# Six of eight setup stages moved into the attention loop of a one-core transformer block, and the softmax shift split into two factors

## The reference, cut to what matters

```python
def attention(x, Wqkv_w, Wqkv_b, U, Wo_w):        # x: (1, 4096, 256), 16 heads of 16
    proj = quant4(x) @ ternary_weight(Wqkv_w).T + Wqkv_b
    q = proj.reshape(B, N, h, dk).transpose(0, 2, 1, 3)
    k = proj.reshape(B, h, N, dk)
    v = proj.reshape(B, h, N, dk)
    q, k = rotary(q, N), rotary(k, N)
    att = einsum('bhnr,bhmr->bhnm', q @ U, k @ U) / sqrt(dk)
    y = (softmax(att) @ v).transpose(0, 2, 1, 3).reshape(B, N, d)
    return quant4(y) @ ternary_weight(Wo_w).T
x = layernorm(x + attention(x))
x = layernorm(x + ffn(x))                         # silu gate, two gelu layers of 1024, back to 256
```

## Time and profile before

| | |
|---|---|
| median of 3 runs | 2857.3 us (2856.99 to 2858.01) |
| the profiled execution, its own time | 2857.96 us |
| its span (first to last instruction) | 2856.3 us |
| granted TensorE clock, mean | 0.966 of full speed |
| busy: PE / DVE / ACT / POOL | 88% / 21% / 74% / 11% of the span |
| setup, up to the first score matmul | 0 to 262.4 us |
| attention, up to the last sum | 262.4 to 2144.8 us |
| check of the sums and feed-forward part | 2144.8 to 2856.3 us |

### The profile page before, as it was taken

One profiled execution on the slowest core, in us unless ns is written; L12 is line 12 of the kernel. 1 busy time (PEld: TensorE's weight loads), 2 busy tenths in 40 slices (PEclk: granted clock), 3 DMA queues, 4 the chain that ended last, 5 costly groups with the idle time before them and its releaser, 6 DMA issues.

```text
span 2856.3 us, 40002 instructions
## 1 busy us (share of the span) xinstructions
PE 2508.4 (88%) x15895; PEld 1048.4 (37%) x15895; DVE 610.1 (21%) x1164; ACT 2124.8 (74%) x2360; POOL 311.4 (11%) x277
## 2 busy tenths in 40 slices
PE   2432999999999999999999999999995999999998
PEld 2220222222222222222222222222224888888887
DVE  7870000000000000000000000000005555655653
ACT  1222999999999999999999999999992223222232
POOL 2442888500000000000000000000000000000000
PEclk9765999999999999999999999999997999999999
DMA  1438444433333233323323333332222011001100
GB/s 60 130 119 228 103 99 104 93 64 63 64 63 67 58 63 63 71 64 63 62 58 67 64 64 63 69 66 60 59 45 48 1 23 22 22 0 22 22 8 16
DMA packets 94888, 178.42 MB, mean 62 GB/s; under 512 B 30432, under 2 KB 56064, under 8 KB 94208
## 3 DMA queue, kind: packets, MB, share of 16 engines
q1 hardware_dynamic: 90624, 153.05, 24.8%
q0 software_dynamic: 4096, 23.07, 3.0%
HBM read 150.63 MB, written 25.43 MB: 62 GB/s over the span
## 4 chain that ended last, share of the span: by engine, by line
ACT 34%; issue 32%; PE 25%; DVE 6%; DMA 2%; SPq 1%; ACTq 1%; DVEq 0%
ACT PB L270 34%; PE PS L517 16%; PE PS L502 4%; PE PS L529 2%; DVE TD L1060 1%; DMA KSL<-KSD 1%; ACTq L268 1%; PE PS L909 1%; DVE xq L1045 0%; DVE rq L1065 0%; DVE rq L1064 0%; DVE V L1048 0%; DVE khl L1068 0%; SPq L763 0%; DMA QSD<-shr 0%
## 5 line engine op out<-in xcount | busy, mean ns | idle before, releaser
L270 ACT ACTIVATE PB<-PS 128x1024 f32<-128x1024 f32 x2048 | 1877.7, 1237 | 1.4 <-PE PS L236 1.4
L245 PE MATMUL PS<-PB,V 128*17 128x512 f32 x8192 | 1079.3, 599 | 0.3 <-ACT PB L270 0.3
L236 PE MATMUL PS<-QSL,KSL 49*128 49x512 f32 x4096 | 753.6, 446 | 171.1 <-DMA KSL<-KSD 52.3
L236 PEld LDWEIGHTS PS<-QSL,KSL 49*128 49x128 f32 x4096 | 306.0, 185 | 1113.3 <-ACT PB L270 1060.9
L280 DVE STREAM_TRANSPOSE accS<-PS 128x512 f32<-128x512 f32 x32 | 22.9, 717 | 1874.5 <-PE PS L245 1874.5
L592 ACT ACTIVATE hfr<-PS,s 128x512 f32<-128x512 f32 x128 | 86.8, 689 | 300.5 <-PE PS L517 300.4
L245 PEld LDWEIGHTS PS<-PB,V 128*17 128x17 f32 x8192 | 136.0, 95 | 378.6 <-issue 364.1
L517 PE MATMUL PS<-hidden_ar,wh1r 128*128 128x512 f32 x1024 | 237.5, 391 | 0.0
L517 PE MATMUL PS<-hidden_br,wh2r 128*128 128x512 f32 x1024 | 235.3, 390 | 0.0
L517 PEld LDWEIGHTS PS<-hidden_br,wh2r 128*128 128x128 f32 x1024 | 191.7, 188 | 39.4
L517 PEld LDWEIGHTS PS<-hidden_ar,wh1r 128*128 128x128 f32 x1024 | 190.7, 188 | 40.1 <-DVE hfr L681 0.5
(11 more groups left out here) (135 smaller groups left out, 954.2 us busy)
## 6 DMA issues: line engine op xcount, KB each, us to landing
KSL<-KSD SPq DMA_DIRECT2D x256, 256.0 KB, 4.3
KSL<-KSD SPq DMA_DIRECT2D x256, 128.0 KB, 5.0
yq<-in_mlp POOLq DMA_DIRECT2D x44, 256.0 KB, 3.1
QSL<-QSD SPq DMA_DIRECT2D x64, 132.0 KB
QSD<-qhl SPq DMA_DIRECT2D x32, 256.0 KB
KSD<-khl SPq DMA_DIRECT2D x64, 128.0 KB
xg<-in_x SPq DMA_DIRECT2D x8, 512.0 KB, 5.7
QSL<-QSD SPq DMA_DIRECT2D x64, 64.0 KB
```

The costliest lines, as they stand in the source:

```text
L236: ins = pe.matmul(PS[:, 2 * (pair % SLOTS) + e, :], KSL[r, q % 2, s, k * P:(k + 1) * P], QSL[r, b % 2, s, :], start=True, stop=True, tile_ ...
L245: ins = pe.matmul(ACC[i * VW:i * VW + DK + 1, :], V17[:, HT * h + u, c, :], PB[:, (2 * unit + i // 2) % RING, (i % 2) * QW:(i % 2 + 1) * Q ...
L270: act.activation(PB[:, pair % RING, :], PS[:, slot:slot + 2, :].rearrange("p a b -> p (a b)"), ACT.Exp).then_inc(at["probs_ready"], 1)
```

## The change

Groups 0 and 1 are set up as before the attention, and of group 2 the projection, of group 3 the transposed x. The rest is cut into 65 visits and put into the units 6 to 94 of the attention's first query chunk, at most one visit in a unit: on PE between the scores and the sums of the unit. A visit fills one PSUM bank; DVE reads it. Before the attention seven banks are used in turn, in it only bank 7, so that PE waits in each visit until DVE has read the one before.

DVE takes over the copies `qTb`, `rkT` and the higher parts of `qhl` and `khl` from ACT. Squares and root go; ACT takes |.| of the higher parts instead (128x1024, twice a group), which PE sums. The shift becomes this sum for the query row (stored at once) times a constant of the head, -0.04 times the largest such sum of its keys, which goes to a new row of `KSD` and from there by DMAs of its own (`load_consts`) to row 48 of each half of `KSL`. The memsets of `KSL` go. Queries are rotated after the keys' visit KN or KM, no longer right after the projection. Blocks of heads 1, 2, 3 load their first keys late (`KEYS_AT`). The weights come in 44 pieces between the checks, after the last visit.

```diff
+BEFORE = [(XT, 0, 0)]
+for _g in range(2):
+    BEFORE += [(PR, 0, _g), (PR, 1, _g), (XT, 0, _g + 1), (KT_, 0, _g), (KT_, 1, _g), (KG, 0, _g), (KG, 1, _g),
+               (KN, 0, _g)] + [(KM, 0, _g)] * (_g % 2) + [(QT_, 0, _g), (QT_, 1, _g), (QN, 0, _g)]
+BEFORE += [(PR, 0, 2), (PR, 1, 2), (XT, 0, 3)]
+for _g, _u in zip(range(2, NQ), range(-2, 100, 15)):
+    _at = [(_u, PR, 0, _g), (_u + 1, PR, 1, _g), (_u + 4, XT, 0, _g + 1), (_u + 8, KT_, 0, _g), (_u + 9, KT_, 1, _g),
+           (_u + 10, KG, 0, _g), (_u + 11, KG, 1, _g), (_u + 13, KN, 0, _g), (_u + 14, KM, 0, _g), (_u + 17, QT_, 0, _g),
+           (_u + 18, QT_, 1, _g), (_u + 21, QN, 0, _g)]
...
+KEYS_AT, CONSTS_AT = {1: 26, 2: 57, 3: 86}, {1: 29, 2: 60, 3: 89}
...
+        BANKS = (7, 0, 1, 2, 3, 4, 5)
+        bank_number = {use: BANKS[use % len(BANKS)] if use < len(BEFORE) else 7 for use in USE.values()}
...
+        def setup_pe(pe, what, i, g):
+            use = USE[what, i, g]
+            bank = PS[:, bank_number[use], :]
+            if bank_before[use] >= 0:
+                pe.wait_ge(setup_read, bank_before[use] + 1)
...
+        def setup_act(act, what, i, g):
+            if what == KG and i == 1:
+                act.wait_ge(k_high, 2 * g + 2)
...
+                act.activation(sqk[:, :, :], khl[:, 0, :, :].bitcast(F32), ACT.Abs).then_inc(k_abs, 1)
...
+        def setup_dve(v, s, what, i, g):
...
+            v.wait_ge(setup_full, use + 1)
...
+            elif what == PR:
...
+                if i == 1:
...
+                                    ALU.add).then_inc(proj_saved, 1)
+                    v.wait_ge(proj_saved, g + 1)
+                    if g + 1 < NQ:
+                        quantise(v, s, g + 1)
+            elif what == KT_:
+                v.tensor_copy(rkT[:, i, :], bank).then_inc(setup_read, 1)
+            elif what in (KG, QT_):
...
+                v.tensor_copy(hl[:, 0, i, :], bank).then_inc(high, 1)
+                v.wait_ge(high, 2 * g + i + 1)
+                v.tensor_tensor(hl[:, 1, i, :], bank, hl[:, 0, i, :].bitcast(F32), ALU.subtract).then_inc(setup_read, 1)
...
+                if g % 2 == 0:
+                    rotate_queries(v, s, g)
+            elif what == KM:
...
+                v.tensor_scalar(kcr[:, :], ones[0:H, :], kmp[:, H:H + 1], -SHIFT, ALU.mult, ALU.mult).then_inc(consts_ready, 1)
+                rotate_queries(v, s, g)
...
+        def first_pe(pe, at):
+            units = NB_ALL * KT
+            pe.wait_ge(setup_read, len(BEFORE))
...
+            for unit in range(units):
+                pe.wait_ge(at["probs_ready"], 2 * unit + 2)
+                for pair in (2 * unit + 3, 2 * unit + 4):
+                    if pair < 2 * units:
+                        scores_pe(pe, at, 0, pair)
+                if unit in SETUP_AT:
+                    setup_pe(pe, *SETUP_AT[unit])
+                if unit % KT == 0:
+                    pe.wait_ge(at["acc_saved"], unit // KT + 1)
+                sums_pe(pe, at, unit, unit // KT % NBLK)
+        def first_act(act, at):
...
+                if pair % 2 and (pair - 5) // 2 in SETUP_AT:
+                    setup_act(act, *SETUP_AT[(pair - 5) // 2])
...
-            for e in range(2):
-                v.memset(KSL[64 * e + 32:64 * e + 64, :, :, :].bitcast(F32), 1.0).then_inc(slots_set, 1)
...
-            load_weights(pool, True)
...
+            for n in range(WCHUNKS):
+                piece, ready = weight_piece(True, n)
+                pool.dma_start(piece, a["mlp"][:, n * QW:(n + 1) * QW]).then_inc(ready, 16)
```

More of the change, by code:

```diff
@@ L222, in postln_block, with keys_in @@
         K_DVE_F = {True: 50, False: 25}
+        def keys_in(at, n0, q):
+            b, k = divmod(q, QPB)
+            if at is first:
+                return b * 160 + (96 if k < 2 else 160)
+            return n0 * (QPB * 32) + (q // 2 + 1) * 64
         def scores_pe(pe, at, n0, pair):
@@ new lines, in quantise @@
+        def quantise(v, s, g):
+            m = mx[:, g % 2, :, :]
+            src = xg[:, g % 2, :, :]
+            v.wait_ge(x_in[g % 2], 16 * (g // 2) + 16)
+            s.did(v.tensor_reduce(m[:, 0, :], src, AX.X, ALU.max, apply_absolute_value=True))
+            s.settle()
+            maxima(v, s, m)
+            for i in range(TQ):
+                ins = v.tensor_scalar(xq[:, i, :], src[:, i, :], m[:, 1, i:i + 1], 7.0, ALU.mult, ALU.mult)
+            ins.then_inc(x_used, 1)
+            v.wait_ge(x_used, g + 1)
+            if g:
+                v.wait_ge(setup_full, USE[XT, 0, g - 1] + 1)
+            v.tensor_scalar(qb[:, :, :], xq[:, :, :], ROUND, -ROUND, ALU.add, ALU.add).then_inc(q_ready, 1)
+            v.wait_ge(q_ready, g + 1)
@@ new lines, in first_act @@
+        def first_act(act, at):
+            for pair in range(2 * NB_ALL * KT):
+                act.wait_ge(at["scores_ready"], pair + 1)
+                if pair >= RING:
+                    act.wait_ge(at["probs_free"], (pair - RING) // 2 + 1)
+                slot = 2 * (pair % SLOTS)
+                act.activation(PB[:, pair % RING, :], PS[:, slot:slot + 2, :].rearrange("p a b -> p (a b)"),
+                               ACT.Exp).then_inc(at["probs_ready"], 1)
+                if pair % 2 and (pair - 5) // 2 in SETUP_AT:
+                    setup_act(act, *SETUP_AT[(pair - 5) // 2])
@@ new lines, in first_dve, with block_dve @@
+        def first_dve(v, s, at):
+            for unit in range(SETUP_UNITS):
+                if unit in SETUP_AT:
+                    setup_dve(v, s, *SETUP_AT[unit])
+                if unit % KT == KT - 1:
+                    block_dve(v, at, unit // KT)
+            for b in range(SETUP_UNITS // KT, NB_ALL):
+                block_dve(v, at, b)
+        def block_dve(v, at, b):
+            sums = accS[:, :].rearrange("p (b f) -> p b f", f=VW)
+            s = Steps(v, at["dve_step"], 2 * b)
+            v.wait_ge(at["probs_free"], b * KT + KT)
+            if b > 0:
+                v.wait_ge(at["y_ready"], b)
+            v.transpose(accS[:, :], ACC).then_inc(at["acc_saved"], 1)
+            v.wait_ge(at["acc_saved"], b + 2)
+            s.did(v.reciprocal(rl[:, :], sums[:, :, DK]))
+            s.did(v.tensor_copy(LS[:, b, :], sums[:, :, DK]))
+            s.settle()
+            if b >= YS:
+                v.wait_ge(at["y_out"][b % YS], b // YS * 16)
+            v.tensor_tensor(Y[:, b % YS, :, :], sums[:, :, 0:DK], rl[:, :].unsqueeze(2).to_broadcast([P, H, DK]),
+                            ALU.mult).then_inc(at["y_ready"], 1)
@@ L742, in _ @@
                 sp.dma_start(W[:, k, :, :], a[w].rearrange("(c p) d -> p c d", p=P)).then_inc(weights_in, 16)
[L743 to L774, removed]
+            load_x(sp, 0)
@@ new lines, in _ @@
+            load_x(sp, 1)
+            for v in BEFORE:
+                store_setup(sp, *v)
+                if v == (KM, 0, 1):
+                    for g in range(2):
+                        sp.wait_ge(k_out[g], 128)
+                    for q in range(2):
+                        load_keys(sp, first, q)
+                    sp.wait_ge(consts_out[0], 16)
+                    for q in range(2):
+                        load_consts(sp, first, q)
+                if v == (QN, 0, 0):
+                    sp.wait_ge(q_out[0], 64)
+                    sp.wait_ge(qn_out[0], 16)
+                    load_queries(sp, first, 0, 0)
@@ L775, in _ @@
+            first_sp(sp, first)
             with sp.If(sums_left_range(sp)):
@@ L811, in _ @@
             pool.memset(same[:, :], 1.0).then_inc(pool_step, 1)
[L812 to L816, removed]
-            load_weights(pool, True)
[L819 to L823, removed]
+            pool.wait_ge(setup_read, len(USE))
@@ L830, in check @@
                 pool.tensor_tensor(same[:, :], same[:, :], wc[k], ALU.mult).then_inc(pool_step, 1)
[L831 to L840, removed]
+                pool.wait_ge(pool_step, step + 4)
@@ L882, in turn @@
-            def turn(bank, src, ready):
-                for half in range(2):
-                    for i in range(TQ):
-                        ins = pe.transpose(PS[:, bank + half, i * P:(i + 1) * P],
-                                           src[:, i, 8 * half:8 * half + 8, :].rearrange("p a f -> p (a f)"), ident[:, :])
-                ins.then_inc(ready, 1)
-            def norms(src, ready):
-                for half in range(2):
-                    ins = pe.matmul(PS[0:H, 6, :], nbk[:, half, :], src[:, half, :], start=half == 0, stop=half == 1)
-                ins.then_inc(ready, 1)
@@ L920, in _ @@
-            pe.wait_ge(kn_saved, NQ)
-            pe.transpose(MISC[0:H, 0:H], kmp[:, 0:H], ident[0:H, 0:H]).then_inc(kmax_T, 1)
-            pe.wait_ge(setup_done, 1)
-            attend_pe(pe, first, 0, NB_ALL, 0)
+            for v in BEFORE:
+                setup_pe(pe, *v)
+            first_pe(pe, first)
             pe.wait_ge(sums_checked, 2)
@@ L1101, in _ @@
-            v.nop().then_inc(setup_done, 1)
+            s = Steps(v, dve_s)
```

(5 more changed lines are left out.)

406 lines of the change are left out of this document (225 added, 181 removed).

## The result

The changed kernel takes 2772.8 us (median of 4 runs, 2771.75 to 2776.77) against 2857.3 before: a ratio of 0.9706, interval 0.969 to 0.9723. The profiled execution took 2776.77 us with a span of 2774.9. The profiled execution was the slowest of the four, 4 us above their median, so lengths read from its trace carry some microseconds of chance.

The account below looks back on a forecast made before the run. ACT's exps bound attention, PE close behind (1.71 of 1.83 us a unit), after 262.4 us of setup. Starting 155 us earlier but lasting 95 longer gives 2797 us; range 2748 to 2838, own range 2775 to 2822.

Parts of the forecast that it names:

- The start: Setup before attention: two groups, the constant and group 3's quantising let attention start at 107 us instead of 262.4, gaining 155.
- Rival (a): DVE's quantising is not slowed by POOL: start at 95 us, attention 62 us longer, 2752 us in all; chance 0.2.
- PE's work in 65 visits: Attention: 47 us of added PE work, of which 8 fit in PE's room of 0.12 us a unit; +39 us.
- stands before the second query half: Groups 3 to 6: PE waits while DVE quantises before reading the first query half; four times 8.2 us, +33.
- projection halves behind the rotation: Groups 3 and 5: DVE's rotation makes it read the next projection halves late, 2 us each; +4 us.
- keys of the second block: Block 1: split, stores, loads and landing take 17.5 us, with some 16 us until first use; +3 us (0 to 8).
- clock behind the stands: After each of four PE stands the granted clock falls to half, costing 2.5 us each; +10 us (0 to 20).
- magnitudes on ACT: Attention: twelve added ACT operations of 0.91 us, 11 us, half hidden while PE is late; +6 us.
- The price of a switch between tilings: Each visit's switch to full-array products between score and sum tiles: 0 to 0.15 us, 0 to 10 in all; taken as 0.
- The rival on the slow side: PE waits in each visit for all of DVE's work, 25.4 us a group, 152 for six; 2900 us; chance 0.05.
- Rival (c): The single bank costs more in every visit, 1.2 us of wait on average instead of 0.77; 2826 us; chance 0.13.
- Rival (b): Magnitudes switch ACT's tables, two loads of 1.28 us for each of twelve, +31 us; 2828 us; chance 0.07.

Follow-up runs that it names:

- pool_late: Changed kernel, but POOL starts rotating the keys of groups 3 to 6 only once DVE has quantised the next x; 2755.4 us, ratio 0.9639 to before.
- quant_moved: Changed kernel, but in attention DVE quantises the next x behind the queries' sum row, transpose of x eight units later; 2742.7 us, ratio 0.9596 to before.
- no_magnitudes: Changed kernel with a nop in place of ACT's twelve magnitude operations beside the attention (groups 2 to 7); 2768.5 us, ratio 0.9685 to before.
- keys_product_twice: Changed kernel with each of the twelve KG products (keys times U) beside the attention done twice on PE; 2786.0 us, ratio 0.9746 to before.

## Why the prediction was right

**The start**, forecast at 107 us, came at 106.0: V of groups 0 and 2 saved at 29.7 and 95.2 us for 29.5 and 95.4, and 10.8 us from there to the first score for 11. A hit within 1 us is luck, as the first score lay anywhere in 3.5 us with the same code. The prediction took the reading that single-source operations wait for POOL like those with two inputs, and pool_late shows POOL as the cause. Its working was rougher than its sum: it had six waits of 1.16 us, and the rows show five of about 0.95, at L246 and the four scalings; the reciprocal did not wait. 9.2 us were forecast, 8.7 came.

The Trainium skill (SBUF - State Buffer, "SBUF: two separate sides") makes the shared port pair an exclusive lock; the trace agrees for the scalings (1.35 us for 0.35) and for an operation on four numbers a partition (1.09 for 0.14).

Rival (a), 2752 us, is out.

**The attention** was forecast 94.7 us longer and is 76.7. Term by term:

| term | forecast | measured or worked out | from |
|---|---|---|---|
| PE's work in 65 visits | 39 | about 30, worked out | below |
| stands before the second query half | 33 | 25.7 | PE's idle rows |
| projection halves behind the rotation | 4 | 3.3 | PE L400, twice |
| keys of the second block | 3 | 3.9, by another path | PE's idle row |
| clock behind the stands | 10 | about 8.6, worked out | quant_moved: 31.9 less 25.7 of stands, and 2.4 for keys |
| magnitudes on ACT | 6 | 4.6 to 8 | no_magnitudes |

The column sums to 76 to 80, of 76.7. As two terms are worked out and the trace is one execution, that they meet so closely is in part chance. The keys' 3 us are luck too: the prediction added up the path of the keys and left out that of the constants, which ended last.

The forecast was 24 us too long: some 18 in the attention, 1 in the start and 2 behind the attention; the rest is that the profiled execution was 4 us above the median.

**The term that was mis-sized** is PE's. The step "PE's unit is 0.66 from the first score to the first sum and 1.05 us of sums" took the modelled end of the sums as the time at which the next scores can start. Where PE is the bound, the rows show otherwise (timeline of the changed kernel):

```profile
159.83 0.74 PE L271 MATMUL PS<-QSL,KSL 49*128 49x512 f32 x4
...
161.48 0.73 PE L271 MATMUL PS<-QSL,KSL 49*128 49x512 f32 x4
...
163.69 0.73 PE L271 MATMUL PS<-QSL,KSL 49*128 49x512 f32 x4
```

A unit without a visit is 1.65 us, not 1.71, so 0.19 us are free instead of 0.12; and one with a sum over heads (161.48 to 163.69) 2.21, the visit 0.56, in the same way 0.55 for a projection half. The key and query transposes, taken at 0.85 from rows at half clock, cost 0.59 (124.10 to 126.33, less 1.64); the products with U 1.06, more than the 0.89 taken. In all 24x0.59 + 12x1.06 + 12x0.56 + 10x0.55 + 4x0.56 + 3x0.16 = 42 us, less 65x0.19 = 12, is 30; the 24 units between the visits can take up 4.6 us more at most. keys_product_twice shows that PE's work counts nearly in full there. Against the forecast the transposes make 6 us less, the larger room 5 and the sums over heads 2; the products with U take back 2 and the projection halves 1.

**The stands** were forecast at 8.2 us each. Two are 8.5, one is 7.0; the second is only 1.75, because it begins 4 us behind the end of the wait for keys, in which DVE quantised on. Two waits that I added overlap. The price of a switch between tilings, taken as nothing, was not seen apart; the 0.2 us by which a product with U costs more than its own length may hold it, and that was not tried.

The rival on the slow side, PE in turn with DVE from 1.7 us a visit, had its place right and not its reach: waits behind DVE were 29 us in 65 visits, 0.45 each. Rival (c), 1.2 us of wait on average, did not come either: stands, clock, projection and keys make 41.5 us, 0.64 a visit where the forecast had 0.77. Rival (b) is out, no table is loaded in attention. That attention ran once is seen from 2048 exps.

## What to carry to other kernels

Work moved beside a saturated loop is not free when the second engine has little room: price it at the loop's own pace, where that engine is the bound. Here the overlap gained 177 us for 76. Then look at the moved work's order in each in-order queue: DVE's cost 32 us and SP's 7 to 10. The first was regained by moving the quantising to where DVE's queue is idle, the second by issuing the loads ahead of stores that wait for DVE. When several loads fill one tile, ask which lands last: here it was the smallest, as its data made a round trip through DRAM behind the others. Waits on one path are not added before it is asked whether one hides the other.

## What the runs showed of the hardware

A stand of PE of 3.44 us was enough for the granted clock to be at 0.50 behind it (pool_late), as after 8.49 us (changed kernel); full clock came back within about 6 us in both, sooner than the nine at the start of attention. Even the stands of 1.66 and 1.65 us before a projection half were followed by half clock in the changed kernel (0.56 in 186 to 188 us; the row below), while in quant_moved one of 1.67 us at 171.41 was not (1.00 from 170 to 176), nor one of 2.08 us in pool_late. So the length of a stand does not decide by itself.

```profile
275.00:278.00 3.00, 3.00 (x13) 0.65 (x12) 2.79 (x4) 0.29 (x1) 0.64 (x1) 0.50 0.86 182
```

DVE's rotation with POOL idle is at its undisturbed length in every instance (changed kernel, durations in ns, min/median/max), where rows 7 had a median of 1775 for the same products. The scalings of the quantising have changed places with it:

```profile
L458 DVE TENSOR_TENSOR TD<-V,rotq x32: 668/673/682, 49.1 to 349.9; 128x512 f32<-128x512 f32 x32
...
L442 DVE TENSOR_SCALAR xq<-xg,mx x32: 347/1350/1431, 21.7 to 283.9; 128x256 f32<-128x256 f32 x32
```
